# A one-core transformer block: four score banks and two banks for transposed probabilities in the last batch's heads, four buffers of probabilities and maxima

## The chip, the cores and the metric

The kernel runs on one core of a Trainium2 chip. The metric is device time in microseconds (us) of one execution, lower is better. TensorE does the matrix products and the transposes and writes only to PSUM, which has 8 banks of 128 partitions x 512 float32 values. VectorE (DVE), ScalarE (ACT) and GpSimd (POOL) work on SBUF; DVE and ACT also read PSUM. The engines run side by side, each in its own fixed order, and meet at semaphores.

## The reference

Eight batches of 512 tokens x 128 channels go through a linear attention block with an MLP, an 8-expert feed-forward, an 8-head causal attention, and at the end a 16-head attention whose values and output projections are chosen per token and head among 8 experts. The change concerns this last part:

```python
q = jnp.einsum('btc,hdc->bhtd', x, Wq)          # 16 heads of 64
k = jnp.einsum('btc,hdc->bhtd', x, Wk)
v = jnp.einsum('bthe,bted->bhtd', mix_v, proj_v)
scores = jnp.einsum('bhid,bhjd->bhij', q * scale, k)
probs = jax.nn.softmax(scores, axis=-1)
attn = jnp.einsum('bhij,bhjd->bihd', probs, v)
...
res = jnp.einsum('bthe,bthd,efd->bthf', mask_o, attn, Wo)
return res.sum(axis=2)
```

All of it is float32. Each batch of 512 tokens is attended over as a whole here.

## The kernel before, in words

The work of a batch is cut into stages. "Front" stages (attn0, moe_in, experts, attn1, gates) compute everything up to the top-2 gates; then come "values" (the mixed values of all heads, on POOL and DVE) and the heads themselves: "begin", "heads", "finish", "close". `schedule` writes the stages of two batches interleaved: the heads of batch b-1 run beside the fronts of batch b. For this the 8 PSUM banks are split by hand: `F0` to `F3` (banks 0 to 3) belong to the front, `S0`, `S1` (banks 4, 5) hold scores, `TB` (bank 6) holds transposed probabilities and `OB` (bank 7) the outputs of the heads. The last batch has no front beside its heads, so that from the end of its values to the end of the program `F0` to `F3` are unused.

The heads stage is a list of steps, `HEAD_STEPS`. The 512 queries are taken in NT = 4 chunks of 128, the 16 heads of a chunk in pairs, so that there are 64 head steps (x = 16 i + h) and, between them, these other steps: "queries" (before heads 4 and 8 of chunks 0 to 2: the projected queries of the next chunk), "back" (before head 14, and before head 6 of the next chunk: the outputs of 8 heads are transposed back), "mixed" (before head 10: outputs through the mask to the experts, read back from memory as `onR`), "result" (before head 12: output projection). Every step that is not "rest" takes the next score bank; `TURN` counts them. All three engines walk the same list in the same order, at different distances behind it:

- TensorE in step k: at an even head x it waits with `free` for the two banks that it is about to write and computes the scores of heads x and x+1 (two matrix products, from the upper and lower 64 partitions); for other steps, their own product. Then, in the same step, it transposes the probabilities of step k-2 (four 128x128 transposes into `TB`), which wait for the exponentials (`s_out`) and for the bank (`pT_r`). Then, when step k-3 is an odd head, it multiplies the transposed probabilities of that pair with the values ("PV" below: 16 small products into `OB`).
- ACT in step k: copies the outputs `OB` to `oaT` after each fourth head; copies `TB` to `prT` for the head of step k-2; then, for a head, computes the exponentials from the score bank into `pr`, with the maximum as bias and the row sums into `den`.
- DVE in step k: finishes "back" and "result" of step k-1, then reduces the score bank of a head to the negated maximum `nmax`.

So with plain steps alone TensorE's order for heads x, x+1 (x even) is: scores x and x+1; transposes of x-2; PV of x-4 and x-3; transposes of x-1. When another step stands before each pair, as from head 4 on in chunks 1 and 2, the order is: that step's product; transposes of x-2; scores x, x+1; transposes of x-1; PV of x-2 and x-1. `free(b, turn)` is the wait for a score bank: its last user was `turn - 2`.

Of the kernel before, what the change touches and what calls it, by code (L numbers as in the profile page):

```python
# [8 lines left out]
ALU = mybir.AluOpType  # L9
# [3 lines left out]
P = 128  # L13
# [17 lines left out]
MIXED_AT = 10  # L31
RESULT_AT = 12
# [22 lines left out]

def values_v(b):
    return LAST_VALUES_V if isinstance(b[0], int) and sum(b) == NB - 1 else VALUES_V
# [67 lines left out]
def build(nc, a, row_table, out):  # L125
    ctx = ExitStack()
    with ctx:
# [123 lines left out]
        nmax = sb("nmax", [P, 2])  # L251
        pr = sb("pr", [P, 2, T])
# [14 lines left out]
        F0, F1, F2, F3, S0, S1, TB, OB = bank  # L267

# [445 lines left out]
        def _(pe):  # L714
# [235 lines left out]
            def free(b, turn):  # L950

                if turn > 2:
                    before = TURN.index(turn - 2)
                    what, y = HEAD_STEPS[before]
                    if what == "result":
                        wait(pe, xout_r, b, y + 1)
                    elif what == "back":
                        wait(pe, on_r, b, y + 1)
                    else:
                        wait(pe, s_out, b, COPIED[before])  # L960

            def steps(b, first, end):


                for k in range(first, end):
                    kind, x, turn = step_of(k)
                    bank_k = (S0, S1)[turn % 2]
# [9 lines left out]
                    if kind == "head" and x % 2 == 0:  # L977
                        i, p = x // HS, x % HS // 2
                        j, r = 2 * i + p // (NP // 2), p % (NP // 2)
                        if r == 0:  # L980
                            wait(pe, s_out, b, COPIED[STEP_AT["queries", j]])
                        for odd in range(2):
                            half = slice(DS * odd, DS * odd + DS)
                            pe.matmul((S0, S1)[(turn + odd) % 2][:, :], qs[half, j % 3, r, :], keys[half, p, :], start=True, stop=True).then_inc(s_ps[0], 1)  # L984
# [20 lines left out]
                    if kind == "head":  # L1005
                        wait(pe, s_out, b, COPIED[k - 2])
                        if m >= 1:
                            wait(pe, pT_r, b, m)
                        transposes(TB, lambda j: pr[:, m % 2, j * P:(j + 1) * P]).then_inc(p_T[0], 1)
# [22 lines left out]
        def _(s):  # L1032
# [138 lines left out]
            def steps(b, first, end):  # L1171
                for k in range(first, end):
# [7 lines left out]
                    if kind == "head":  # L1180
                        wait(s, p_T, b, m + 1)
                        s.activation(prT[:, m % 3, :], TB[:, :], ACT.Copy).then_inc(pT_r[0], 1)  # L1182
                    kind, x, turn = step_of(k)
                    bank_k = (S0, S1)[turn % 2]
# [3 lines left out]
                    if kind == "head":  # L1188
                        wait(s, nmax_r, b, x + 1)
                        if x >= 2:  # L1190
                            wait(s, p_T, b, x - 1)
# [3 lines left out]
                        s.activation(pr[:, x % 2, :], bank_k[:, :], ACT.Exp, bias=nmax[:, x % 2:x % 2 + 1], accum_out=den[:, i % 2, h:h + 1]).then_inc(s_out[0], 1)  # L1195
# [15 lines left out]
        def _(v):  # L1211
# [289 lines left out]
            def steps(b, first, end):  # L1501
                for k in range(first, end):
                    kind, m, _ = step_of(k - 1)
                    if kind == "result":
                        wait(v, s_ps, b, TURN[k - 1])
                        v.tensor_tensor(xout[:, m, :], (S0, S1)[TURN[k - 1] % 2][:, 0:P], xout[:, m, :], ALU.add).then_inc(xout_r[0], 1)
                    kind, m, turn = step_of(k - 1)
                    if kind == "back":
# [5 lines left out]
                        v.tensor_tensor(on[:, half, :], (S0, S1)[turn % 2][:, :].rearrange("p (h d) -> p h d", d=DS), rden[:, m % 2, :].unsqueeze(2).to_broadcast([P, HS // 2, DS]), ALU.mult).then_inc(on_r[0], 1)  # L1514
                    kind, m, turn = step_of(k)
                    if kind == "head":
                        wait(v, s_ps, b, turn)
                        if m >= 2:
                            wait(v, s_out, b, COPIED[STEP_AT["head", m - 2]])
                        v.tensor_reduce(nmax[:, m % 2:m % 2 + 1], (S0, S1)[turn % 2][:, :], X_AXIS, ALU.max, negate=True).then_inc(nmax_r[0], 1)  # L1520
# [40 lines left out]
```

## Time and profile before

| | |
|---|---|
| median of 3 runs | 3037.46 us (3032.28 to 3060.35) |
| profiled execution, its own time | 3036.23 us |
| span of its profile | 3034.4 us |
| mean granted TensorE clock | 0.924 |
| busy: PE / DVE / ACT / POOL | 82% / 52% / 45% / 26% |
| last batch: end of its values on DVE, first exponential | 2847.6 us, 2848.33 us |
| last batch: scores of the last pair | 3009.28 us |

The span is the time from the first to the last instruction; 1.8 us lie around it. Busy shares are means over stages that are bound by different things, so the rows that follow the next section are of one stage, from 2848 us to the end. In a row, the first number is the start in us, the second how long it took; several equal instructions that follow each other are one row (x4), and brackets give the idle time before it and what ended that idle time. Line numbers are those of the kernel before: L984 is the scores, L1520 the maxima, L1195 the exponentials, L717 all transposes of whole tiles (here of `pr`), L1182 the copy to `prT`, L1021 PV, L975 queries, L988 back, L996 mixed, L1002 result.

### The profile page before, as it was taken

The numbers are of one execution on the slowest core, as the hardware profiler recorded it, in microseconds if no ns is written. First come the engines' busy times: TensorE is split into PE (matmuls) and PEld (weight loads), VectorE is DVE, ScalarE is ACT, GpSimd is POOL, SyncE is SP. The second block draws the span as 40 slices with busy tenths as digits, with TensorE's granted clock in tenths as the row PEclk, the third lists the DMA queues.
The fourth block names the chain that finished last, engine by engine and source line by source line (L and its number), as shares of the span: only waits on it lengthen the run. The fifth ranks groups of instructions, "written<-read, shape, count | busy, mean of one in ns | idle before, by whom it ended". The sixth has DMA issues, their size and how long they took to land.

```text
span 3034.4 us, 45348 instructions
## 1 busy us (share of the span) xinstructions
PE 2497.6 (82%) x15660; PEld 1535.7 (51%) x15660; DVE 1565.5 (52%) x2646; ACT 1361.4 (45%) x2925; POOL 803.4 (26%) x370
## 2 busy tenths in 40 slices
PE   3984699879897898889898798978988898986476
PEld 2353346554475445654365544754456544754254
DVE  4235753456635484464835565364834557337632
ACT  0232226463364525554265634555255633643254
POOL 1002620015501191013700164011900147004500
PEclk7996799999899998999899998999989999998798
DMA  2110010102010030102101030101201121001001
GB/s 75 42 49 9 9 54 1 50 22 67 22 38 20 25 78 2 43 28 47 44 1 56 15 77 12 43 15 43 60 2 43 29 56 33 15 15 40 0 29 32
DMA packets 210741, 101.69 MB, mean 34 GB/s; under 512 B 137369, under 2 KB 189622, under 8 KB 210494
## 3 DMA queue, kind: packets, MB, share of 16 engines
q1 hardware_dynamic: 205052, 95.74, 11.4%
q10 hardware_dynamic: 5440, 2.75, 0.3%
q8 instruction: 143, 2.34, 0.3%
q14 instruction: 106, 0.85, 0.1%
HBM read 77.48 MB, written 20.99 MB: 32 GB/s over the span
## 4 chain that ended last, share of the span: by engine, by line
issue 42%; PE 34%; POOL 10%; DVE 7%; ACT 6%; DMA 1%; ACTq 0%; POOLq 0%; DVEq 0%
POOL prod L702 7%; PE bank L717 6%; PE bank L984 5%; PE bank L829 4%; PE bank L832 4%; PE bank L1021 3%; PE bank L837 3%; ACT prT L1182 2%; ACT pr L1195 2%; POOL rstd L641 1%; PE bank L869 1%; DVE nrm_o L1294 1%; PE bank L996 1%; DVE prod L1477 1%; PE bank L885 1%
## 5 line engine op out<-in xcount | busy, mean ns | idle before, releaser
L702 POOL TENSOR_TENSOR prod<-pv,mixv 128x1024 f32<-128x1024 f32 x184 | 608.3, 3344 | 243.3 <-ACT pv L1146 170.5
L1520 DVE TENSOR_REDUCE nmax<-bank 128x1 f32<-128x512 f32 x512 | 340.6, 687 | 608.1 <-PE bank L984 605.6
L1182 ACT ACTIVATE prT<-bank 128x512 f32<-128x512 f32 x512 | 305.6, 597 | 611.2 <-PE bank L717 607.3
L984 PE MATMUL bank<-keys,qs 64*128 64x512 f32 x1024 | 318.0, 698 | 220.1 <-ACT pr L1195 92.4
L641 POOL TENSOR_TENSOR rstd<-vareps,minus_half 128x4 f32<-128x4 f32 x48 | 50.0, 1042 | 1323.7 <-DVE vareps L1289 1323.6
L1195 ACT ACTIVATE pr<-bank,nmax 128x512 f32<-128x512 f32 x512 | 349.5, 685 | 98.3 <-DVE nmax L1520 97.3
L717 PE MATMUL bank<-ident,pr 128*128 128x128 f32 x2048 | 351.7, 298 | 36.1 <-ACT prT L1182 35.9
L717 PEld LDWEIGHTS bank<-ident,pr 128*128 128x128 f32 x2048 | 241.8, 150 | 270.1 <-issue 217.1
L1088 ACT ACTIVATE arena<-bank 128x512 f32<-128x512 f32 x256 | 152.8, 597 | 469.3 <-PE bank L829 429.4
L1021 PE MATMUL bank<-prT,vals 128*64 128x128 f32 x4096 | 299.5, 292 | 63.0 <-ACT prT L1182 63.0
L1485 DVE TENSOR_REDUCE vals<-prod 128x128 f32<-128x1024 f32 x256 | 306.6, 1208 | 35.9 <-POOL prod L702 35.9
L1378 DVE TENSOR_TENSOR arena<-bank,arena 128x512 f32<-128x512 f32 x256 | 175.1, 686 | 245.2 <-PE bank L832 230.9
L1021 PEld LDWEIGHTS bank<-prT,vals 128*64 128x64 f32 x4096 | 235.8, 145 | 115.4 <-ACT prT L1182 72.7
L832 PE MATMUL bank<-h1T,Wu 128*128 128x512 f32 x512 | 268.4, 606 | 19.0 <-DVE arena L1378 19.0
L1406 DVE TENSOR_REDUCE nmax<-bank 128x1 f32<-128x128 f32 (+3 forms) x256 | 125.7, 491 | 282.9 <-PE bank L870 282.2
L829 PE MATMUL bank<-h1T,Wg 128*128 128x512 f32 x512 | 266.2, 602 | 0.9 <-ACT h1T L1053 0.9
L837 PE MATMUL bank<-arena,Wd 128*128 128x512 f32 x512 | 263.6, 600 | 2.8 <-DVE arena L1378 2.4
L984 PEld LDWEIGHTS bank<-keys,qs 64*128 64x128 f32 x1024 | 84.3, 197 | 281.3 <-ACT pr L1195 113.2
L869 PE MATMUL bank<-arena,attT 128*128 128x512 f32 (+3 forms) x512 | 198.9, 473 | 4.4 <-ACT arena L1116 3.0
L1477 DVE TENSOR_TENSOR prod<-pv,mixv 128x1024 f32<-128x1024 f32 x72 | 179.7, 2495 | 0.0
L832 PEld LDWEIGHTS bank<-h1T,Wu 128*128 128x128 f32 x512 | 97.6, 193 | 147.1 <-issue 113.2
L885 PEld LDWEIGHTS bank<-v,arena 128*128 128x128 f32 x1280 | 165.8, 194 | 1.0 <-issue 1.0
(220 smaller groups left out, 3077.1 us busy)
## 6 DMA issues: line engine op xcount, KB each, us to landing
Wg<-in_L_ffn_Wg SPq DMA_DIRECT2D x64, 256.0 KB, 2.8
Wu<-in_L_ffn_Wu SPq DMA_DIRECT2D x64, 256.0 KB, 3.1
Wd<-in_L_ffn_Wd SPq DMA_DIRECT2D x64, 256.0 KB, 3.8
out_rows<-on SPq DMA_DIRECT2D x32, 512.0 KB, 2.6
onR<-out_rows SPq DMA_DIRECT2D x32, 512.0 KB, 3.8
xin<-in_L_attn_x SPq DMA_DIRECT2D x8, 256.0 KB, 4.2
mask_rows<-masko SPq DMA_DIRECT2D x8, 256.0 KB, 4.3
maskR<-mask_rows SPq DMA_DIRECT2D x8, 256.0 KB, 6.6
```

The source lines that it names most:

```text
L702: g.tensor_tensor(*value_piece(n), ALU.mult).then_inc(vprod_r[0], 1)
L717: last = pe.transpose(dst[:, i * P:(i + 1) * P], src(i), ident[:, :])
L829: pe.matmul(F0[:, :], Wg[:, e % 2, j * P:(j + 1) * P], hbT[:, :], start=True, stop=True).then_inc(gu_g[0], 1)
L832: pe.matmul((F2, F3)[n % 2][:, :], Wu[:, e % 2, j * P:(j + 1) * P], hbT[:, :], start=True, stop=True).then_inc(gu_u[0], 1)
L837: pe.matmul(F1[:, :], Wd[:, e % 2, j, :], act[:, m % 3, :], start=(m == 0), stop=(m == n_all - 1)).then_inc(down_ps[0], 1)
L869: pe.matmul(f[:, 0:w], q1T[:, i * P:(i + 1) * P], k1z[:, h, 0:w], start=True, stop=False, skip_group_check=True)
L984: pe.matmul((S0, S1)[(turn + odd) % 2][:, :], qs[half, j % 3, r, :], keys[half, p, :], start=True, stop=True).then_inc(s_ps[0], 1)
L1021: last = pe.matmul(OB[DS * odd:DS * odd + DS, at:at + P], vals[:, j, h - 1 + odd, :], prT[:, (m - 1 + odd) % 3, j * P:(j + 1) * P], start= ...
L1182: s.activation(prT[:, m % 3, :], TB[:, :], ACT.Copy).then_inc(pT_r[0], 1)
L1195: s.activation(pr[:, x % 2, :], bank_k[:, :], ACT.Exp, bias=nmax[:, x % 2:x % 2 + 1], accum_out=den[:, i % 2, h:h + 1]).then_inc(s_out[0], 1)
L1485: v.tensor_reduce(vals[:, i, HQ * q:HQ * q + HQ, :], prod[:, m % NPROD, :].rearrange("p (h d e) -> p h d e", h=HQ, e=NE), X_AXIS, ALU.add) ...
L1520: v.tensor_reduce(nmax[:, m % 2:m % 2 + 1], (S0, S1)[turn % 2][:, :], X_AXIS, ALU.max, negate=True).then_inc(nmax_r[0], 1)
```

## The change

For the last batch alone (`is_last`), the score turns go round four banks, `S0, S1, F0, F1`, in place of two, and the transposed probabilities alternate between `TB` and `F2`. `free` then waits for the user of four turns ago, and the transposes wait for the copy of two heads ago. For all batches `pr` and `nmax` have four buffers in place of two, and the waits that guard them reach back four heads. Work, order of the instructions on each engine, and sizes are unchanged; `prT` (three buffers) and `OB` are as before.

```diff
--- before.py
+++ after.py
@@ -29,6 +29,7 @@
 QUERIES_AT = (4, 8)
 BACK_AT = (14, 6)
 MIXED_AT = 10
+NPR = 4
 RESULT_AT = 12
 BUILD_BEFORE = 4
 
@@ -53,8 +54,13 @@
 LAST_VALUES_V = [n for n in range(NQ * NT) if n % 2]
 
 
+def is_last(b):
+
+    return isinstance(b[0], int) and sum(b) == NB - 1
+
+
 def values_v(b):
-    return LAST_VALUES_V if isinstance(b[0], int) and sum(b) == NB - 1 else VALUES_V
+    return LAST_VALUES_V if is_last(b) else VALUES_V
 
 
 def by_pool(n, by_v):
@@ -248,8 +254,8 @@
 
         keys = sb("keys", [P, NP, T])
         qs = sb("qs", [P, 3, NP // 2, P])
-        nmax = sb("nmax", [P, 2])
-        pr = sb("pr", [P, 2, T])
+        nmax = sb("nmax", [P, 4])
+        pr = sb("pr", [P, 4, T])
         prT = sb("prT", [P, 3, T])
         oaT = sb("oaT", [P, NP, P])
         den = sb("den", [P, 2, HS])
@@ -265,6 +271,14 @@
 
         bank = [ctx.enter_context(nc.psum_tensor(f"bank{i}", [P, T], F32)) for i in range(8)]
         F0, F1, F2, F3, S0, S1, TB, OB = bank
+
+        def score_banks(b):
+
+            return (S0, S1, F0, F1) if is_last(b) else (S0, S1)
+
+        def probs_banks(b):
+
+            return (TB, F2) if is_last(b) else (TB,)
 
         def tiles(t):
             return t[:, :].rearrange("p (i c) -> p i c", i=NT)
@@ -949,8 +963,9 @@
 
             def free(b, turn):
 
-                if turn > 2:
-                    before = TURN.index(turn - 2)
+                ahead = len(score_banks(b))
+                if turn > ahead:
+                    before = TURN.index(turn - ahead)
                     what, y = HEAD_STEPS[before]
                     if what == "result":
                         wait(pe, xout_r, b, y + 1)
@@ -962,9 +977,10 @@
             def steps(b, first, end):
 
 
+                S, TP = score_banks(b), probs_banks(b)
                 for k in range(first, end):
                     kind, x, turn = step_of(k)
-                    bank_k = (S0, S1)[turn % 2]
+                    bank_k = S[turn % len(S)]
                     if kind == "head":
                         for odd in range(0 if x % 2 else 2):
                             free(b, turn + odd)
@@ -981,7 +997,7 @@
                             wait(pe, s_out, b, COPIED[STEP_AT["queries", j]])
                         for odd in range(2):
                             half = slice(DS * odd, DS * odd + DS)
-                            pe.matmul((S0, S1)[(turn + odd) % 2][:, :], qs[half, j % 3, r, :], keys[half, p, :], start=True, stop=True).then_inc(s_ps[0], 1)
+                            pe.matmul(S[(turn + odd) % len(S)][:, :], qs[half, j % 3, r, :], keys[half, p, :], start=True, stop=True).then_inc(s_ps[0], 1)
                     if kind == "back":
                         wait(pe, oa_r, b, NBACK * (x + 1))
                         for p in range(NJ):
@@ -1004,9 +1020,9 @@
                     kind, m, turn = step_of(k - 2)
                     if kind == "head":
                         wait(pe, s_out, b, COPIED[k - 2])
-                        if m >= 1:
-                            wait(pe, pT_r, b, m)
-                        transposes(TB, lambda j: pr[:, m % 2, j * P:(j + 1) * P]).then_inc(p_T[0], 1)
+                        if m >= len(TP):
+                            wait(pe, pT_r, b, m - len(TP) + 1)
+                        transposes(TP[m % len(TP)], lambda j: pr[:, m % NPR, j * P:(j + 1) * P]).then_inc(p_T[0], 1)
                     kind, m, turn = step_of(k - 3)
                     if kind == "head" and m % 2:
                         i, h = m // HS, m % HS
@@ -1169,6 +1185,7 @@
                 yield from steps(b, CLOSE_AT, len(HEAD_STEPS) + 1)
 
             def steps(b, first, end):
+                S, TP = score_banks(b), probs_banks(b)
                 for k in range(first, end):
                     kind, m, _ = step_of(k - 4)
                     if kind == "head" and m % GROUP == GROUP - 1:
@@ -1179,20 +1196,20 @@
                     kind, m, _ = step_of(k - 2)
                     if kind == "head":
                         wait(s, p_T, b, m + 1)
-                        s.activation(prT[:, m % 3, :], TB[:, :], ACT.Copy).then_inc(pT_r[0], 1)
+                        s.activation(prT[:, m % 3, :], TP[m % len(TP)][:, :], ACT.Copy).then_inc(pT_r[0], 1)
                     kind, x, turn = step_of(k)
-                    bank_k = (S0, S1)[turn % 2]
+                    bank_k = S[turn % len(S)]
                     if kind == "queries":
                         wait(s, s_ps, b, turn)
                         s.activation(qs[:, x % 3, :, :].rearrange("p a t -> p (a t)"), bank_k[:, :], ACT.Copy).then_inc(s_out[0], 1)
                     if kind == "head":
                         wait(s, nmax_r, b, x + 1)
-                        if x >= 2:
-                            wait(s, p_T, b, x - 1)
+                        if x >= NPR:
+                            wait(s, p_T, b, x - NPR + 1)
                         i, h = x // HS, x % HS
                         if h == 0 and i >= 2:
                             wait(s, rden_r, b, 2 * (i - 1))
-                        s.activation(pr[:, x % 2, :], bank_k[:, :], ACT.Exp, bias=nmax[:, x % 2:x % 2 + 1], accum_out=den[:, i % 2, h:h + 1]).then_inc(s_out[0], 1)
+                        s.activation(pr[:, x % NPR, :], bank_k[:, :], ACT.Exp, bias=nmax[:, x % NPR:x % NPR + 1], accum_out=den[:, i % 2, h:h + 1]).then_inc(s_out[0], 1)
                     if kind == "mixed":
                         wait(s, s_ps, b, turn)
                         if x:
@@ -1499,11 +1516,12 @@
                 yield from steps(b, CLOSE_AT, len(HEAD_STEPS) + 1)
 
             def steps(b, first, end):
+                S = score_banks(b)
                 for k in range(first, end):
                     kind, m, _ = step_of(k - 1)
                     if kind == "result":
                         wait(v, s_ps, b, TURN[k - 1])
-                        v.tensor_tensor(xout[:, m, :], (S0, S1)[TURN[k - 1] % 2][:, 0:P], xout[:, m, :], ALU.add).then_inc(xout_r[0], 1)
+                        v.tensor_tensor(xout[:, m, :], S[TURN[k - 1] % len(S)][:, 0:P], xout[:, m, :], ALU.add).then_inc(xout_r[0], 1)
                     kind, m, turn = step_of(k - 1)
                     if kind == "back":
                         half = slice(HS // 2 * (m % 2), HS // 2 * (m % 2) + HS // 2)
@@ -1511,13 +1529,13 @@
                         v.reciprocal(rden[:, m % 2, :], den[:, m // 2 % 2, half]).then_inc(rden_r[0], 1)
                         wait(v, rden_r, b, m + 1)
                         wait(v, s_ps, b, turn)
-                        v.tensor_tensor(on[:, half, :], (S0, S1)[turn % 2][:, :].rearrange("p (h d) -> p h d", d=DS), rden[:, m % 2, :].unsqueeze(2).to_broadcast([P, HS // 2, DS]), ALU.mult).then_inc(on_r[0], 1)
+                        v.tensor_tensor(on[:, half, :], S[turn % len(S)][:, :].rearrange("p (h d) -> p h d", d=DS), rden[:, m % 2, :].unsqueeze(2).to_broadcast([P, HS // 2, DS]), ALU.mult).then_inc(on_r[0], 1)
                     kind, m, turn = step_of(k)
                     if kind == "head":
                         wait(v, s_ps, b, turn)
-                        if m >= 2:
-                            wait(v, s_out, b, COPIED[STEP_AT["head", m - 2]])
-                        v.tensor_reduce(nmax[:, m % 2:m % 2 + 1], (S0, S1)[turn % 2][:, :], X_AXIS, ALU.max, negate=True).then_inc(nmax_r[0], 1)
+                        if m >= NPR:
+                            wait(v, s_out, b, COPIED[STEP_AT["head", m - NPR]])
+                        v.tensor_reduce(nmax[:, m % NPR:m % NPR + 1], S[turn % len(S)][:, :], X_AXIS, ALU.max, negate=True).then_inc(nmax_r[0], 1)
                     if k in BUILD_AT:
                         i = BUILD_AT[k]
                         wait(v, mask_in, b, 16)
```

TensorE, chunk 0, heads 10 to 13 of the last batch. Before:

```order
L984 MATMUL bank5<-keys,qs 128x512 [waits s_out]
L984 MATMUL bank4<-keys,qs 128x512
L717 MATMUL bank6<-ident,pr 128x128 [waits pT_r,s_out]
L717 MATMUL bank6<-ident,pr 128x128 x3
L717 MATMUL bank6<-ident,pr 128x128 [waits pT_r,s_out]
L717 MATMUL bank6<-ident,pr 128x128 x3
L984 MATMUL bank5<-keys,qs 128x512 [waits s_out]
L984 MATMUL bank4<-keys,qs 128x512
L717 MATMUL bank6<-ident,pr 128x128 [waits pT_r,s_out]
L717 MATMUL bank6<-ident,pr 128x128 x3
L1021 MATMUL bank7<-prT,vals 64x128 [waits pT_r,oa_r]
L1021 MATMUL bank7<-prT,vals 64x128 x7
```

After:

```order
L1000 MATMUL bank1<-keys,qs 128x512 [waits s_out]
L1000 MATMUL bank4<-keys,qs 128x512
L731 MATMUL bank6<-ident,pr 128x128 [waits pT_r,s_out]
L731 MATMUL bank6<-ident,pr 128x128 x3
L731 MATMUL bank2<-ident,pr 128x128 [waits pT_r,s_out]
L731 MATMUL bank2<-ident,pr 128x128 x3
L1000 MATMUL bank5<-keys,qs 128x512 [waits s_out]
L1000 MATMUL bank0<-keys,qs 128x512
L731 MATMUL bank6<-ident,pr 128x128 [waits pT_r,s_out]
L731 MATMUL bank6<-ident,pr 128x128 x3
L1037 MATMUL bank7<-prT,vals 64x128 [waits pT_r,oa_r]
L1037 MATMUL bank7<-prT,vals 64x128 x7
```

The sequence is the same. The scores now alternate through four banks, so that the `s_out` wait at the first row of a pair is for an older exponential; the transposes alternate between banks 6 and 2.

ACT, the first heads of the last batch. Before:

```order
L1195 ACTIVATE pr,den<-bank5,nmax 128x512 [waits nmax_r]
L1195 ACTIVATE pr,den<-bank4,nmax 128x512 [waits nmax_r]
L1182 ACTIVATE prT<-bank6 128x512 [waits p_T]
L1195 ACTIVATE pr,den<-bank5,nmax 128x512 [waits p_T,nmax_r]
L1182 ACTIVATE prT<-bank6 128x512 [waits p_T]
L1195 ACTIVATE pr,den<-bank4,nmax 128x512 [waits p_T,nmax_r]
L1182 ACTIVATE prT<-bank6 128x512 [waits p_T]
L1187 ACTIVATE qs<-bank5 128x512 [waits s_ps]
```

After:

```order
L1212 ACTIVATE pr,den<-bank1,nmax 128x512 [waits nmax_r]
L1212 ACTIVATE pr,den<-bank4,nmax 128x512 [waits nmax_r]
L1199 ACTIVATE prT<-bank6 128x512 [waits p_T]
L1212 ACTIVATE pr,den<-bank5,nmax 128x512 [waits nmax_r]
L1199 ACTIVATE prT<-bank2 128x512 [waits p_T]
L1212 ACTIVATE pr,den<-bank0,nmax 128x512 [waits nmax_r]
L1199 ACTIVATE prT<-bank6 128x512 [waits p_T]
L1204 ACTIVATE qs<-bank1 128x512 [waits s_ps]
```

The order of copies and exponentials is the same; the first exponentials no longer wait for transposes (`p_T`), and the copies read two banks in turn.

## Rows read from the trace of the kernel before

**Rows 1.** Windows of the last batch's heads: each engine's busy time, granted clock.

```profile
core 0: us, PE busy (x) PEld busy (x) DVE busy (x) ACT busy (x) POOL busy (x), PEclk, DMA share, GB/s
2850.00:2884.85 34.85, 27.26 (x217) 16.87 (x217) 9.82 (x16) 19.62 (x47) 0.00 (x0) 0.95 0.00 1
2884.85:2927.93 43.08, 32.48 (x320) 21.92 (x321) 13.34 (x22) 22.80 (x55) 0.00 (x0) 1.00 0.09 26
...
2971.00:3009.28 38.28, 29.53 (x280) 19.39 (x281) 12.05 (x20) 20.15 (x48) 0.00 (x0) 0.96 0.10 29
```

**Rows 2.** Waits between 2850 and 3010 us, the three of TensorE that matter.

```profile
engine line waited for: us in total, times, longest us
PE bank L984 <- ACT pr L1195: 38.1, 12, 28.7
...
PE bank L1021 <- ACT prT L1182: 13.2, 18, 0.8
...
PE bank L717 <- ACT prT L1182: 6.1, 9, 0.8
```

**Rows 3.** Timeline of one pair of heads, from its scores to the next scores.

```profile
start us, us, engine line op out<-in xcount [idle before <-releaser]
2870.80 1.13 PE L984 MATMUL bank<-keys,qs 64*128 64x512 f32 x4 [0.34 <-ACT pr L1195]
...
2871.86 0.66 PE L717 MATMUL bank<-ident,pr 128*128 128x128 f32 x4
2871.94 1.29 DVE L1520 TENSOR_REDUCE nmax<-bank 128x1 f32<-128x512 f32 x2 [2.54 <-PE bank L984]
2872.56 0.60 ACT L1182 ACTIVATE prT<-bank 128x512 f32<-128x512 f32 x1 [1.62 <-PE bank L717]
2873.05 0.68 ACT L1195 ACTIVATE pr<-bank,nmax 128x512 f32<-128x512 f32 x1
...
2873.30 0.63 PE L717 MATMUL bank<-ident,pr 128*128 128x128 f32 x4 [0.78 <-ACT prT L1182]
...
2874.46 0.68 ACT L1195 ACTIVATE pr<-bank,nmax 128x512 f32<-128x512 f32 x1
...
2875.38 1.13 PE L984 MATMUL bank<-keys,qs 64*128 64x512 f32 x4 [1.45 <-ACT pr L1195]
```

**Rows 4.** Timeline of TensorE, two places where it runs without a wait.

```profile
2880.04 1.09 PE L1021 MATMUL bank<-prT,vals 128*64 128x128 f32 x16
...
2881.06 1.13 PE L984 MATMUL bank<-keys,qs 64*128 64x512 f32 x4
...
2882.12 0.65 PE L717 MATMUL bank<-ident,pr 128*128 128x128 f32 x4
...
2936.61 0.63 PE L717 MATMUL bank<-ident,pr 128*128 128x128 f32 x4
...
2937.17 1.09 PE L1021 MATMUL bank<-prT,vals 128*64 128x128 f32 x16
```

**Rows 5.** Timeline of the start of the last batch's heads.

```profile
2848.33 0.69 ACT L1195 ACTIVATE pr<-bank,nmax 128x512 f32<-128x512 f32 x1 [28.31 <-DVE nmax L1520]
...
2849.92 2.08 PE L984 MATMUL bank<-keys,qs 64*128 64x512 f32 x4 [28.72 <-ACT pr L1195]
...
2851.92 1.11 PE L717 MATMUL bank<-ident,pr 128*128 128x128 f32 x4
```

**Rows 6.** Timeline of the tail: from a chunk's transposed outputs through memory to its mixing.

```profile
3017.22 0.63 PE L988 MATMUL bank<-ident,oaT 128*128 128x128 f32 x4 [0.57 <-ACT oaT L1178]
...
3025.05 3.63 PE L996 MATMUL bank<-spread,onR 128*64 128x32 f32 x64 [7.21 <-DMA onR<-out_rows]
```

**Rows 7.** Timeline of TensorE at the lower clock, in the fourth chunk.

```profile
2975.59 1.50 PE L984 MATMUL bank<-keys,qs 64*128 64x512 f32 x4 [1.45 <-ACT pr L1195]
...
2977.02 1.11 PE L717 MATMUL bank<-ident,pr 128*128 128x128 f32 x4
...
2978.07 1.84 PE L1021 MATMUL bank<-prT,vals 128*64 128x128 f32 x16
```

**Rows 8.** A window of batch 7's front beside batch 6's heads.

```profile
2600.00:2650.00 50.00, 48.88 (x443) 37.19 (x442) 19.14 (x34) 32.42 (x78) 0.00 (x0) 1.00 0.08 23
```

**Rows 9.** Timeline of the last two heads' transposes.

```profile
3012.80 0.66 PE L717 MATMUL bank<-ident,pr 128*128 128x128 f32 x4
...
3014.24 0.63 PE L717 MATMUL bank<-ident,pr 128*128 128x128 f32 x4 [0.78 <-ACT prT L1182]
```


## The prediction, made before the run

> **What bounds the kernel now.** I read the page first, then only the stretch that the change touches: the heads of the last batch, which run with no front beside them. The windows of that stretch [rows 1] cut it from 2850 us (just after the first exponentials) to 3009.28 us (the scores of the last pair), by chunks. The third chunk, 2927.93 to 2971.00, has the same numbers as the second within 0.01 us. The reader is to see two things. TensorE is the busiest engine in every window, yet not full: 27.26 of 34.85, twice 32.48 of 43.08, and 29.53 of 38.28 us, in all 121.75 of 159.28 us, so it is idle for 37.5 us. And ACT (22.80 of 43.08) and DVE (13.34) have far more room. So nothing here is bound by one engine's work; it is bound by TensorE's waits.
>
> The waits say which [rows 2]. TensorE waits for the copy to `prT` before PV 18 times, 13.2 us in all (0.73 each), and before transposes 9 times, 6.1 us. The wait of the scores for exponentials is 38.1 us with one wait of 28.7 us in it, which lies before 2850; 9.4 us are left. That is 28.7 of the 37.5 us; the other 8.8 are waits of the scores for the other users of the two banks (queries, mixed, back), which the windows' idle time contains.
>
> One pair of heads shows the mechanism [rows 3]. The scores start at 2870.80, a transpose at 2871.86, its copy at 2872.56, the exponential at 2873.05. The next transposes are ready to go but `TB` is full: idle 0.78 us until the copy is through. The second exponential starts at 2874.46, and only 0.92 us after that, at 2875.38, do the next scores start: both banks had to be empty, idle 1.45 us. The pair took 4.58 us.
>
> **What the change does to this.** The order on each engine stays, so I can walk it with the durations of the trace. Where TensorE does not wait, the steps from start to start are [rows 4]: PV to scores 1.02, scores to transposes 1.06, transposes to what follows 0.56. A plain pair (scores, transposes, PV, transposes) is then 1.06 + 0.56 + 1.02 + 0.56 = 3.20 us. Can the others follow?
> - Scores of x+2 need, with four banks, the exponential of x-1, which is more than a pair old. No wait.
> - Transposes of x need the exponential of x. With scores at 0, the maxima start at 1.14 and take 0.65 each [rows 3]. Transposes of x-2 at 1.06, copy at 1.76 (0.70 later), exponential at 2.25 (0.49 later), TensorE can go on 0.92 later: 3.17. In the order its turn comes at 3.20 + 1.06 = 4.26. For x+1: its maximum ends at 2.44; transposes of x-1 at 2.64, copy 3.34, exponential 3.83, ready at 4.75; its turn comes at 5.84. Where plain pairs follow a pair that had another step before it, the copies lag and the margin shrinks to about 0.1 us, but it is there.
> - ACT's loop (transposes, copy, exponential, transposes two heads later) is 0.70 + 0.49 + 0.92 = 2.11 us for two heads, under 3.20.
>
> So **TensorE becomes the bound** and the waits for score banks and for `TB` go: 9.4 + 6.1 + 8.8 = 24.3 us. **What stays** is the wait before PV. With another step before each pair the order is transposes of x-1, then at once PV of x-2 and x-1, which needs the copy of just those transposes. No bank helps: 0.70 to the copy's start and as much again until it is read. These are the 18 waits of 13.2 us. By my count of the step list they stand at the same places after the change: 3 in chunk 0, 6 each in chunks 1 and 2, 3 in the fourth up to its last pair, so 18.
>
> **A new wait** can come from the mixing. In the tail, where nothing hides it, 7.83 us pass from the start of the back-transposes to the mixed product, through two DMAs [rows 6]. In the fourth chunk the work of TensorE between the two is, after the change, 0.5 (back) + 0.56 + 1.02 + 1.06 + 1.41 (transposes, wait, PV) + 1.02 + 1.06 + 0.56 + 0.5 = 7.7 us (back-transposes taken like others, 0.5 to 0.56), so 0.1 us of wait. In chunks 1 and 2 queries (8 transpose-sized products, 1 us) and one more PV wait lie there too: over 9 us, no wait.
>
> **The start** gains on its own [rows 5]. The first scores are long done while DVE finishes the values; the first exponential starts at 2848.33. Before, the second pair of scores waits for both, starts at 2849.92 and takes 2 us at the lower clock, and the first transposes follow at 2851.92. With four banks these scores have run in the idle time before, and the transposes can start at 2848.33 + 0.92 = 2849.25: 2.7 us.
>
> **The end** gains a little [rows 9]: the last transposes waited 0.78 us for `TB` and started 1.44 after those before them; 0.56 would do. 0.9 us. What comes after (PV, back, two DMAs, mixed, result, store) is a chain of latencies that the change leaves.
>
> **The clock.** In the fourth chunk TensorE ran a spell at 1.2 GHz: scores 1.50, transposes 1.11, PV 1.84 us [rows 7] against 1.13, 0.66 and 1.09 [rows 3, 4], 1.57 us in all, after a wait of 1.45 us. The two middle chunks have none (granted 1.00, [rows 1]) with the same pattern of waits, so I can't tell from the rows what causes it. With TensorE denser I count it as gone: 1.6 us; if it stays the sum is less by that. A stretch with TensorE busy for 48.88 of 50 us has the granted clock at 1.00 [rows 8], so density as such does not lower it.
> The Trainium skill has a rule that speaks against the change: "TensorE: Matmul & The Clock Gate", section "A second HAM failure mode: psum-queue depth-cycling", tells of a kernel that cycled through PSUM banks and left TensorE idle for moments between groups, so that the clock went to and fro between its two levels. By that rule each chunk would show spells like the one above. The trace does not bear it out so far: 0.95 to 1.00 granted with a quarter of the time idle [rows 1].
>
> **All other batches.** `pr` and `nmax` with four buffers change nothing. ACT's copy of head x-2 already waits for the transposes that the old guard named, one instruction ahead of the exponential, and DVE's wait for the scores already implied the exponential of two heads ago. No instruction is added, so 0; on either side I allow 2 us over six batches.
>
> **Sum.** 24.3 - 0.1 + 2.7 + 0.9 + 1.6 = 29.4 us. From the profiled execution's 3036.23 us: 3006.8, so **3007 us**. That execution lies 1.2 us under the median of 3037.46. It is 1.0% off the median, just where a measurement of this kernel begins to tell a gain from no change (about 1%, here 3007.1 us).
>
> **Rivals.**
> 1. *Margins are used up.* In plain pairs the transposes have 0.1 us in hand, DVE's `on` (0.69 us) and the spreading of the mask stand ahead of maxima, and semaphores of two engines meet. If TensorE waits 0.25 us in 48 of the 64 heads, 12 us come back: 3019. For it: the walk uses single rows. Against it: the rows repeat to 0.01 us from chunk to chunk.
> 2. *The clock as in the skill's rule.* One spell of 1.6 us in each of four chunks in place of one in all: 3006.8 + 1.6 + 4 x 1.6 = 3015.
> 3. *The change does nothing*, because the queue in order holds each score back behind PV and the transposes, which wait anyhow: 3036. Against it: the scores themselves wait 18 us beyond what stands before them.
> 4. *More goes than I say*: the waits before PV too, as bound: 37.5 + 2.7 + 0.9 + 1.6 = 43, so 2994. Against it: transposes and PV of the same head are neighbours in the order.
> 5. *Slower.* Denser work brings the clock down in earnest, in this stretch. The 121.75 us of TensorE's work grow by as much as the share of time at 1.2 GHz; at 24% the gain of 29 is eaten; at half they add 61 us, and 3007 becomes 3068. Against it: [rows 8].
>
> **How the numbers follow.** The forecast (3000 to 3014) gets 0.60, a little over half of it, 0.34, under 3007.1. Rival 1 gets 0.17, rival 2 0.08, rival 3 0.05, rival 4 0.06, rival 5 0.04. Faster by over 1%: 0.34 + 0.06 = 0.40. Slower: 0.04. Within 1%: the rest, 0.56. The range takes in the forecast and rivals 1 and 2 with their spread of a few us, and leaves out 3, 4 and 5: 2998 to 3021.
>
> **What the profile after would show.** Waits of the scores for exponentials, queries, mixed and back near zero in the last batch; no wait of transposes for `prT` there; 18 or 19 waits of PV of 0.7 us as before. Plain pairs 3.2 us apart; chunks 1 and 2 near 36.7 us in place of 43.1. First transposes at about 1 us after the first exponential. The stretches of batches 0 to 6 unchanged. What would make me wrong: transposes that wait for exponentials (rival 1), a granted clock under 0.9 in these windows (2 and 5), or a difference that arises in the other batches.

## The result, and the profile after

| | before | changed |
|---|---|---|
| median | 3035.43 us (4 runs, 3032.28 to 3060.35) | 3003.90 us (4 runs, 3000.33 to 3011.61) |
| profiled execution, own time / span | 3036.23 / 3034.4 us | 3002.54 / 3000.7 us |
| first exponential of the last batch | 2848.33 us | 2844.55 us |
| from it to the end of the span | 186.07 us | 156.15 us |

The ratio is 0.9899, with a 95% interval of 0.9853 to 0.9944 (the two medians alone divide to 0.9896). A repetition of the changed kernel beside a later experiment, with 6 runs, gave a median of 3000.09 us and 0.9884 (0.9862 to 0.9906). The kernel is faster, by 1.0 to 1.2%.

The last two rows of the table separate the change from the rest: up to the first exponential of the last batch the two programs issue the same work, but for one pair of scores that the changed kernel computes in the idle time before it; the rest of the change lies behind it. Of the 33.7 us between the spans, 29.9 arise there and 3.8 before it. In the changed kernel L1000 is the scores, L731 transposes, L1199 the copy to `prT`, L1212 exponentials, L1037 PV, L1012 mixed, L1538 maxima.

The windows of the changed kernel's last batch, from the first exponential on, cut at the first scores of each chunk and at the scores of the last pair:

```profile
core 0: us, PE busy (x) PEld busy (x) DVE busy (x) ACT busy (x) POOL busy (x), PEclk, DMA share, GB/s
2844.55:2872.94 28.39, 25.39 (x213) 17.93 (x213) 10.29 (x17) 20.24 (x51) 0.00 (x0) 0.92 0.00 1
2872.94:2909.26 36.32, 31.87 (x322) 21.67 (x320) 13.34 (x22) 22.47 (x57) 0.00 (x0) 1.00 0.11 31
2909.26:2945.31 36.05, 31.66 (x322) 21.66 (x321) 13.34 (x22) 22.48 (x57) 0.00 (x0) 1.00 0.10 30
2945.31:2976.26 30.95, 27.01 (x282) 18.26 (x280) 11.61 (x20) 19.19 (x49) 0.00 (x0) 1.00 0.12 35
2976.26:3000.70 24.44, 11.23 (x125) 9.03 (x124) 4.04 (x7) 4.60 (x10) 0.00 (x0) 0.70 0.18 54
```

And two windows of the kernel before, cut at the same places; those between them are in [rows 1]:

```profile
2848.33:2884.85 36.52, 27.35 (x217) 16.99 (x217) 10.38 (x17) 21.06 (x51) 0.00 (x0) 0.93 0.00 1
...
3009.28:3034.40 25.12, 11.42 (x124) 9.02 (x124) 3.61 (x6) 4.24 (x10) 0.00 (x0) 0.73 0.18 53
```

Stretch by stretch: 36.52 became 28.39 us, 43.08 became 36.32, 43.09 became 36.05, 38.26 became 30.95, and the tail 25.12 became 24.44. TensorE is now busy for 31.87 of 36.32 us in the second chunk, where it was 32.48 of 43.08 [rows 1].

TensorE's waits in this stage, the counterpart of [rows 2] (idle us in total, times, longest):

```profile
engine line waited for: us in total, times, longest us
...
PE bank L731 <- ACT pr L1212: 27.2, 1, 27.2
...
PE bank L1037 <- ACT prT L1199: 14.7, 20, 0.8
...
PE bank L1012 <- ACT pr L1212: 1.7, 1, 1.7
```

The first row is the wait for the first exponential, which ends the values stage. The wait of scores for exponentials and that of transposes for the copy are gone. Twenty waits before PV stay, 18 of them up to the last pair, as before; the sum of those 18 is 13.2 us in both kernels.

A pair of heads, the counterpart of [rows 3], TensorE alone. Scores, transposes, PV, transposes, back, with no bracket behind any of them, that is, no idle time:

```profile
2864.27 1.13 PE L1000 MATMUL bank<-keys,qs 64*128 64x512 f32 x4
...
2865.33 0.66 PE L731 MATMUL bank<-ident,pr 128*128 128x128 f32 x4
...
2865.91 1.09 PE L1037 MATMUL bank<-prT,vals 128*64 128x128 f32 x16
...
2866.94 0.66 PE L731 MATMUL bank<-ident,pr 128*128 128x128 f32 x4
...
2867.43 0.60 PE L1004 MATMUL bank<-ident,oaT 128*128 128x128 f32 x4
```

Where nothing stands between two pairs, their scores start 3.26 us apart (2947.39 and 2950.65 us, in the fourth chunk); the prediction had 3.20, and the pair of [rows 3] took 4.58.

The start, the counterpart of [rows 5]: TensorE goes on 0.83 us after the first exponential, with transposes; its second pair of scores had been computed long before.

```profile
2844.55 0.69 ACT L1212 ACTIVATE pr<-bank,nmax 128x512 f32<-128x512 f32 x1 [28.42 <-DVE nmax L1538]
...
2845.38 1.97 PE L731 MATMUL bank<-ident,pr 128*128 128x128 f32 x8 [27.21 <-ACT pr L1212]
```

### The profile page after: what moved, and what is told of

The parts are those of the page before. It is cut to its first block and busy times, and to the rows that moved or that the text cites. A ratio compares the mean times of both kernels' runs of the same rounds, so it can differ in the third digit from the quotient of the medians.

```text
span 3000.7 us, 45314 instructions
## 1 busy us (share of the span) xinstructions
PE 2487.5 (83%) x15660; PEld 1534.4 (51%) x15660; DVE 1566.4 (52%) x2646; ACT 1359.2 (45%) x2925; POOL 803.1 (27%) x370
## 5 line engine op out<-in xcount | busy, mean ns | idle before, releaser
L1538 DVE TENSOR_REDUCE nmax<-bank 128x1 f32<-128x512 f32 x512 | 340.3, 686 | 572.2 <-PE bank L1000 571.4
L1199 ACT ACTIVATE prT<-bank 128x512 f32<-128x512 f32 x512 | 305.7, 597 | 581.4 <-PE bank L731 578.1
L1000 PE MATMUL bank<-keys,qs 64*128 64x512 f32 x1024 | 314.7, 693 | 171.5 <-ACT pr L1212 54.3
L731 PE MATMUL bank<-ident,pr 128*128 128x128 f32 x2048 | 349.2, 297 | 56.5 <-ACT prT L1199 29.3
L1212 ACT ACTIVATE pr<-bank,nmax 128x512 f32<-128x512 f32 x512 | 349.9, 686 | 98.2 <-DVE nmax L1538 97.3
L731 PEld LDWEIGHTS bank<-ident,pr 128*128 128x128 f32 x2048 | 241.9, 150 | 285.9 <-issue 198.9
L1037 PE MATMUL bank<-prT,vals 128*64 128x128 f32 x4096 | 296.7, 290 | 63.0 <-ACT prT L1199 63.0
L1037 PEld LDWEIGHTS bank<-prT,vals 128*64 128x64 f32 x4096 | 233.6, 143 | 114.6 <-ACT prT L1199 73.6
L1000 PEld LDWEIGHTS bank<-keys,qs 64*128 64x128 f32 x1024 | 83.0, 195 | 230.9 <-ACT pr L1212 72.0
L1126 ACT ACTIVATE arena<-bank 128x128 f32<-128x128 f32 (+3 forms) x256 | 112.1, 438 | 122.3 <-PE bank L731 121.5
```

What stands on the lines that cost most here:

```text
L731: last = pe.transpose(dst[:, i * P:(i + 1) * P], src(i), ident[:, :])
L1000: pe.matmul(S[(turn + odd) % len(S)][:, :], qs[half, j % 3, r, :], keys[half, p, :], start=True, stop=True).then_inc(s_ps[0], 1)
L1037: last = pe.matmul(OB[DS * odd:DS * odd + DS, at:at + P], vals[:, j, h - 1 + odd, :], prT[:, (m - 1 + odd) % 3, j * P:(j + 1) * P], start= ...
L1199: s.activation(prT[:, m % 3, :], TP[m % len(TP)][:, :], ACT.Copy).then_inc(pT_r[0], 1)
L1212: s.activation(pr[:, x % NPR, :], bank_k[:, :], ACT.Exp, bias=nmax[:, x % NPR:x % NPR + 1], accum_out=den[:, i % 2, h:h + 1]).then_inc(s_o ...
L1538: v.tensor_reduce(nmax[:, m % NPR:m % NPR + 1], S[turn % len(S)][:, :], X_AXIS, ALU.max, negate=True).then_inc(nmax_r[0], 1)
```

## Experiments

The number to compare in each is the time from the first exponential of the last batch to the end of the span ("the stage"): 186.1 us before, 156.2 us changed. Two executions of one kernel differ in it by up to 2.5 us, while the whole times of the changed kernel range from 2994.71 to 3011.61 us (last part of this section).

**The two parts alone.** One keeps the four score banks:

```diff
-            return (TB, F2) if is_last(b) else (TB,)
+            return (TB,)
```

> Four score banks in the last batch as in the changed kernel, but one bank for transposed probabilities. My theory (TensorE becomes the bound, each kind of wait is worth what it measured): only the waits of transposes for the copy come back, 9 to 12 times 0.8 us; from the first exponential of the last batch to the end 156.2 + 7 to 10 us, so about 164 us (186.1 before, 156.2 changed), time about 3012 us. Rival (one bank of transposes binds all of it, the score banks alone are of little use): 175 us or more.

Measured: first exponential at 2846.96 us, span 3009.7, so a stage of 162.7 us. Median 3015.44 us, ratio 0.9940 (0.9917 to 0.9962). Its waits:

```profile
PE bank L1037 <- ACT prT L1199: 14.7, 20, 0.8
PE bank L731 <- ACT prT L1199: 6.9, 10, 0.8
```

The wait of transposes for the copy is back, 10 times, 6.9 us in all, and the stage is 6.6 us longer than with both parts, 0.5 us less than the lower end of my range. The mechanism held and the rival fell, but 6.6 us is too little for the second bank of transposes: in this run the mixed product of the fourth chunk did not wait (it waited 1.70 us in the changed kernel), and the last product, L1018, took 1.13 us at the higher clock and not 2.05. The repetition of the changed kernel below had both of these too (a wait of 0.20 us, and 1.13 us); its stage is 153.8 us, so 9.0 us shorter than this one. A wait of 0.78 us also costs a little more than its idle time: with it, transposes start 1.44 us behind the transposes before them, without it about 0.56 [rows 9, 4].

The other keeps the two banks for transposed probabilities:

```diff
-            return (S0, S1, F0, F1) if is_last(b) else (S0, S1)
+            return (S0, S1)
```

> Two banks for transposed probabilities in the last batch, but two score banks. My theory: the scores still wait for the exponential just before them, and the transposes that are no longer held up only move that wait; the second transposes start up to 0.8 us earlier, their copy and the second exponential with them. 186.1 us from the first exponential to the end becomes 178 to 184. Rival (the two parts are worth their own waits, independent of each other): 6 us less, 180, and together with the other part the sum of both is exactly the gain; if the parts need each other, the two gains add up to less than 29.9 us.

Measured: first exponential at 2846.80, span 3031.3, a stage of 184.5 us, just beyond my range. Median 3031.11 us, ratio 0.9985 (0.9966 to 1.0004).

```profile
PE bank L1000 <- ACT pr L1212: 41.0, 12, 28.7
...
PE bank L991 <- ACT pr L1212: 1.5, 2, 0.9
PE bank L1012 <- ACT pr L1212: 0.9, 1, 0.9
```

No wait of transposes for the copy is left, but the scores wait longer for exponentials: 41.0 us with 28.7 in one wait, so 12.3, against 38.1 - 28.7 = 9.4 in [rows 2]; queries and the mixed product now wait 1.5 and 0.9 us for them too. The kernel before waited 6.9 us for the copy up to the end of the program (the 6.1 of [rows 2] and one more wait in the tail); 5.3 of these have only moved to the banks of the scores, and the other 1.6 are the gain. Alone the parts bring 23.4 and 1.6 us, together 29.9. They are not independent: the second bank for transposes is worth 1.6 us while the scores are held, and 6.6 once they are free (9.0 against the repetition). The 1.6 us by itself is within the scatter of the stage, and the ratio does not tell it from nothing; the waits do. This run also has one spell of lower clock more than the kernel before, in its third chunk, about 1.5 us (last section); even without it the part alone would bring only about 3 us (an estimate).

**The buffers.** One kernel takes the four buffers and neither of the bank changes; one takes both bank changes and two buffers (`NPR = 2`).

> Four buffers of probabilities and maxima, all banks as before. My theory: nothing, in any batch; 186.1 us +- 0.3 from the first exponential of the last batch to the end, and the first exponential between 2844 and 2850 us. Rival (the 3.8 us by which the changed kernel reached that exponential earlier come from these buffers in batches 0 to 6): first exponential at 2844.5 +- 1 here too.

Measured: stage 3031.8 - 2845.19 = 186.6 us, median 3039.29 us, ratio 1.0003 (0.9986 to 1.0020). The stage is 0.5 us longer, a little outside my 0.3; that is the wait for the DMA before the last mixed product, 7.7 us in place of 7.2. Its other waits in the stage are those of the kernel before, to 0.1 us. Its first exponential stands at 2845.19, inside both theories' windows, so that one number does not decide between them. The ratio of ten runs shows no gain, but 3.8 us (0.13%) lie just inside its interval. The other kernels with four buffers have their first exponentials anywhere from 2840.08 to 2853.44 us, and the one with two buffers (next) at 2846.50, so 3.8 us are well within the scatter of the batches before. That the buffers bring nothing there is the likely reading, not a shown one.

> The changed kernel with two buffers of probabilities and maxima in place of four. My theory: the order of the copies and exponentials on ScalarE already implies the guards, so 156.2 us +- 1 from the first exponential to the end; the four buffers are not part of the gain. Rival (with four banks the maxima run ahead and are held by the two buffers): 159 us or more, with waits of the maxima for exponentials.

Measured: 3002.2 - 2846.50 = 155.7 us, median 2997.55 us, ratio 0.9873 (0.9847 to 0.9898). The four buffers have no part in the gain. The reason that I gave holds only in part, though: with two buffers the maxima do wait for exponentials, as the rival said, but so little that TensorE has no wait from it.

```profile
DVE nmax L1538 <- ACT pr L1212: 1.7, 5, 0.3
```

**Three score banks** (`S0, S1, F0`):

> The changed kernel with three score banks (S0, S1, F0) in place of four; two banks for transposed probabilities stay. The scores of heads x and x+1 then need the exponential of x-2, which the transposes right behind them need anyhow. My theory: TensorE has that exponential nearly in time, so 1 to 4 us of the gain is lost: 157 to 160 us from the first exponential to the end (156.2 with four, 184.5 with two). Rival (two more banks are needed since every turn must find its bank empty): 165 us or more.

Measured: 3000.2 - 2840.08 = 160.1 us, at the upper edge of my range. Median 3003.67 us, ratio 0.9900 (0.9875 to 0.9925).

```profile
PE bank L1000 <- ACT pr L1212: 32.3, 5, 28.3
```

With 28.3 us in the wait for the start, four waits of 4.0 us in all remain. The start loses as well: the second pair of scores waits for the first exponential, and the first transposes follow that exponential by 2.93 us (0.83 with four banks). In exchange the mixed product of the fourth chunk waited only 0.3 us here, where it waited 1.7 in the changed kernel, because its read landed sooner. As measured, 24.4 of the 28.3 us that the step from two score banks to four brings come with the third bank. With the changed kernel's wait before the mixed product this stage would be about 161.5 us (an estimate), so that the fourth bank is worth 4 to 5 us. In the medians the two can't be told apart.

**The wait before PV.** This wait was what the prediction said would stay. To take it away, PV of the last batch goes one step later in the list, with the copy of the outputs, and `prT` gets four buffers:

```diff
-        prT = sb("prT", [P, 3, T])
+        prT = sb("prT", [P, 4, T])
...
+        def pv_lag(b):
+
+            return 4 if is_last(b) else 3
...
-                    kind, m, turn = step_of(k - 3)
+                    kind, m, turn = step_of(k - pv_lag(b))
...
-                    kind, m, _ = step_of(k - 4)
+                    kind, m, _ = step_of(k - 1 - pv_lag(b))
```

> The changed kernel, and in the last batch the product with the values comes one step later (and the copy of the outputs with it), with four buffers of transposed probabilities in place of three. My theory: the wait before that product, 18 times 0.73 us, goes, since the copy has a whole step of time; nothing else binds closely, so 156.2 us from the first exponential to the end becomes 143 to 147, time about 2992 us. Rival (the wait moves to the next thing that is late, transposes for exponentials or the mixed product for its DMA, which already waits 1.7 us in the fourth chunk): 150 or more.

Measured: 3004.8 - 2853.44 = 151.4 us, median 2997.97 us, ratio 0.9868 (0.9847 to 0.9890). The waits before PV are gone but for one in the last pair, and 4.8 us with them, not 13. My theory fell, the rival was right. What took their place (exponential; transposes; mixed product):

```profile
2942.47 0.68 ACT L1220 ACTIVATE pr<-bank,nmax 128x512 f32<-128x512 f32 x1
...
2943.30 0.66 PE L739 MATMUL bank<-ident,pr 128*128 128x128 f32 x4 [0.92 <-ACT pr L1220]
...
2965.63 3.46 PE L1020 MATMUL bank<-spread,onR 128*64 128x32 f32 x64 [2.23 <-ACT pr L1220]
```

The transposes wait 0.92 us for their exponential. PV had stood between the previous transposes and these, and its wait had covered theirs. In the whole stage there are now 10 such waits, 6.6 us. The third row is the mixed product of the fourth chunk, which waits 2.2 us for its DMA (0.5 more than in the changed kernel) and then ran at the lower clock, 3.46 us against 2.06 (1.4 more).

The next experiment rests on this reading: PV should neither follow its own transposes nor leave the gap before the next. Two steps later instead of one (`pv_lag` 5, six buffers of `prT`) puts it between scores-and-transposes and the next other step.

> As late_pv, but the product with the values comes two steps later than in the changed kernel, with six buffers of transposed probabilities. It then stands between transposes and the next other step where those steps are dense, and fills the time in which the next exponential is awaited. My theory: both the waits before that product and the 6.6 us of new waits of transposes for exponentials in late_pv go: 144 to 148 us from the first exponential to the end (151.4 in late_pv), a new minimum of about 2993 us. Rival (the mixed product waits longer for its DMA as TensorE gets there earlier, and eats it): 150 or more, with 3 us or more of wait before the mixed product.

Measured: 2986.5 - 2843.92 = 142.6 us, median 2988.06 us, ratio 0.9845 (0.9821 to 0.9869).

```profile
2843.92:2962.00 118.08, 114.14 (x1118) 78.55 (x1118) 48.66 (x81) 83.81 (x207) 0.00 (x0) 0.98 0.10 28
```

```profile
PE bank L739 <- ACT pr L1220: 28.3, 4, 27.2
...
PE bank L1020 <- DMA onR<-out_rows: 7.4, 1, 7.4
...
PE bank L1020 <- ACT pr L1220: 2.2, 2, 1.8
```

TensorE is busy for 114.14 of 118.08 us up to the end of the transposes. Beyond the 27.2 us of the start only 1.1 us of waits for exponentials are left, no wait before PV, and 2.2 us before mixed products. The waits went as the theory said, and the stage came out 1.4 us below its range; the rival fell. This is the fastest kernel of the study.

**How well the numbers repeat.**

> The changed kernel once more, beside later_pv on one chip. My theory: the stage from the first exponential of the last batch to the end repeats at 156 us +- 1.5, while the time of that first exponential scatters by several us from execution to execution with the clock of the batches before; ratio to the kernel before 0.990. Rival (the stage itself scatters as much as the rest, and the gain with it): the stage off by 3 us or more.

Measured: 2998.7 - 2844.93 = 153.8 us. That is 2.4 us off, between what the theory and the rival expected. 1.5 of it is the mixed product of the fourth chunk, whose DMA landed sooner (last section), and 0.9 the last product, L1018, which ran at the higher clock: 1.13 us against 2.05. The ratio, 0.9884 (0.9862 to 0.9906), is a little better than I wrote.

> later_pv once more: 142.6 +- 1.5 us from the first exponential to the end, 13 to 14 us under the changed kernel in the median too.

Measured: 2986.2 - 2846.16 = 140.0 us, median 2990.86 us, ratio 0.9854 (0.9830 to 0.9878). On the same chip the changed kernel had 3000.09, so 9.2 us more, not 13 to 14, while the stages differ by 13.8. The stage is 2.5 us shorter than in the first execution and so outside my 1.5, for the same two reasons: 1.9 us less wait before mixed products, and 0.9 us in the last product. The effect of an order is thus best read between executions that are alike in these two.

## Why the prediction was right

**The bound.** The step on which all rested, that TensorE becomes the bound once scores and transposes find their banks empty, is shown by the windows and by scores_only and probs_only. The walk with single rows gave 36.7 us for chunks 1 and 2; they took 36.32 and 36.05.

**The sum**, 29.4 us from the stage, measured 29.9. By terms:
- Waits for banks, 24.3 us, and the start, 2.7. The first stretch (the start and chunk 0) should gain about 5.4 and 2.7 and gained 8.1. Chunks 1 and 2 had 10.6 us idle with 6 waits of 0.73 to stay, 6.2 to gain, and gained 6.8 and 7.0. The rest is in TensorE's busy time, 32.48 before, 31.87 and 31.66 after, for the same work: a row of scores lasts 1.13 us in the record but the next one starts 1.06 later [rows 4], so busy time shrinks where nothing waits. The walk by starts (36.7) contained part of this, the sum by idle time did not: it is 0.6 and 0.8 us in chunks 1 and 2, and 0.9 in the fourth.
- The lower clock in the fourth chunk, 1.6 us: the window after has the clock at 1.00. The gain is in, and it goes with the score banks: the spell stands in the second pair of this chunk in all three kernels with two score banks (before, buffers_only, probs_only) and there in none of those with three or four. What sets it off stays open (last section). In late_pv a spell came at the mixed product, so that denser work alone does not keep the clock up.
- The wait before the mixed product, 0.1 us: it was 1.7. This term was mis-sized. TensorE's own work between back-transposes and mixed product took 7.66 us, as walked (7.7), but the way through memory took 9.4 us and not the tail's 7.83: the read from memory took 5.3 us, where in the tail before it took 3.7. In the repetition the wait was 0.2.
- The end, 0.9 us: 0.7.
- The fourth chunk thus gained 7.3 where 6.5 + 1.6 - 0.1 = 8.0 was expected. That the whole sum is right to 0.5 us is luck in part: 1.6 us missed here stand against 2.3 us of shorter busy time that it did not count. In the repetition the stage gained 32.3.
- The other batches, 0 with 2 us either way: buffers_only has 1.0003, and two_buffers shows that they bring nothing in the stage either. But I had not allowed for scatter of the batches before: 13 us over these executions. The predicted 3007 against 3003.90 and 3000.09 differs by that more than by anything in the sum.

**What stays.** The 18 waits of 13.2 us before PV stayed to the tenth of a us. That no bank helps is shown by the changed kernel, and that an order does by later_pv. Later_pv also has six buffers of `prT`, which its order needs; that such buffers do nothing in the old order was not run, but argued: PV there waits for the copy of the transposes just ahead of it.

**The rivals.** That margins are used up (rival 1, 12 us) did not happen: in the changed kernel transposes have no wait for exponentials after the start. It did happen in late_pv, where PV no longer gave them time. Rival 2 did not happen: with four banks in turn, the last three chunks ran at a granted clock of 1.00 in the changed kernel. So the Trainium skill's rule ("TensorE: Matmul & The Clock Gate", section "A second HAM failure mode: psum-queue depth-cycling"), that cycling through PSUM banks with short idle moments makes the clock go to and fro, is not borne out by the changed kernel; the five spells in four of the other kernels (last section), each close behind a short idle time, agree with it in part. Rival 5 fell too: in later_pv TensorE is busy for 97% of a stretch of 118 us with a granted clock of 0.98. Rival 3 fell with the result and with scores_only, rival 4 with the waits before PV.

**The chances.** I put 0.40 on a gain of more than 1% and 0.56 on less. The forecast itself leaned the other way, 0.34 of its 0.60 above 1%; what tipped it were rivals 1, 2 and 3, of which none happened. Both measurements lie just above, 1.01 and 1.16%; the interval of the first reaches to both sides.

## What to carry to other kernels

Count TensorE's idle time in a stage and split it by what ended it; a wait that is for an empty bank goes with more banks, one that is for the result of the instruction just ahead in the same queue needs another order. Try buffers in the combination in which the engine behind them can run on: one more bank for transposes was worth 1.6 us alone and 6.6 to 9.0 us once scores were free. Before an instruction is moved away from a wait, look at what its place had covered: one step later won 5 us, two steps 14.

## What the runs showed of the hardware

**The time of one DMA.** The same reading DMA, `out_rows` to `onR`, 512 KB, took from 3.7 to 5.4 us from issue to landing. In the changed kernel's fourth chunk (columns: KB, median us to landing):

```profile
issues: line engine op xcount, KB each, median us to landing
onR<-out_rows SPq DMA_DIRECT2D x1, 512.0 KB, 5.3
```

Beside it TensorE's back-transposes, the issue, and the mixed product:

```profile
2953.81 0.60 PE L1004 MATMUL bank<-ident,oaT 128*128 128x128 f32 x4
...
2957.82 0.37 SPq L592 DMA_DIRECT2D onR<-out_rows  x1
...
2963.17 2.06 PE L1012 MATMUL bank<-spread,onR 128*64 128x32 f32 x64 [1.70 <-ACT pr L1212]
```

2957.82 and 5.3 make 2963.1, and the product starts at 2963.17. So the wait of 1.70 us is for the DMA, though the trace puts it down to `ACT pr`. In the repetition the DMA took 3.8 us and the product waited 0.20:

```profile
2962.25 2.06 PE L1012 MATMUL bank<-spread,onR 128*64 128x32 f32 x64 [0.20 <-issue]
```

Ahead of the tail there are three such transfers in each of the eleven profiled executions. Of these 33, nine took 4.7 to 5.4 us (two each in the changed kernel and two_buffers, one each in probs_only, late_pv, three_banks, later_pv and change_again) and the others 3.7 to 4.2. What lengthens them stays open.

**Spells of lower clock.** Behind the start of the stage and ahead of its tail, the granted clock fell in five places in the eleven executions, each time within about 1.2 us behind an idle time of TensorE of 1.45 to 2.23 us: in the second pair of the fourth chunk before and in buffers_only (1.45 us), in the second pair of the third and of the fourth chunk in probs_only (2.17 us each), and at the mixed product in late_pv (2.23 us). The one of buffers_only:

```profile
2972.47 1.84 PE L1000 MATMUL bank<-keys,qs 64*128 64x512 f32 x4 [1.45 <-ACT pr L1212]
```

The same scores take 1.13 us at the higher clock. But such an idle time is not enough: the second pair of chunk 1 before also waited 1.45 us, and the mixed products of the changed kernel and of later_pv waited 1.70 and 1.82 us, all without a spell. A spell cost 1.4 to 1.6 us. Which of the idle times brings one stays open. In the tail, the last product, which follows an idle time of 0.73 us, ran at the lower clock (2.05 us) in eight of the eleven executions and at the higher one (1.13 us) in scores_only, change_again and later_pv_again.
